# A conditioned transformer block on one core: earlier input, a new first tile, two banks and new orders at the end

## What is computed

```python
def _tc_rmsnorm(x, t, gw, gb, bw, bb):
    g = (t @ gw.T + gb)[:, None, :]
    b = (t @ bw.T + bb)[:, None, :]
    inv_rms = jax.lax.rsqrt(jnp.mean(x * x, axis=-1, keepdims=True) + EPS)
    return g * x * inv_rms + b

def _attention(x, Wq, Wk, Wv, Wo):      # 16 heads of 16
    ...
    p = softmax(q @ k.T / sqrt(dh))
    return (p @ v) @ Wo.T

def _swiglu(x, gate_w, hid_w, out_w):   # 1024 hidden channels
    return jax.nn.silu(x @ gate_w.T) * (x @ hid_w.T) @ out_w.T

x1 = x + _attention(_tc_rmsnorm(x, t, g1w, g1b, b1w, b1b), Wq, Wk, Wv, Wo)
out = x + x1 + _swiglu(_tc_rmsnorm(x1, t, g2w, g2b, b2w, b2b), gate_w, hid_w, out_w)
```

## Time and profile before

| | us |
|---|---|
| median of 3 runs | 942.82 (942.0 to 943.25) |
| the profiled execution | 944.17 |
| span of its instructions | 942.4 |
| TensorE (PE) busy in that span | 898.8, 95% |
| DVE, ACT, POOL busy | 629.0, 553.4, 493.3 |
| mean granted TensorE clock | 0.981 of full speed |

### The profile page before, as it was taken

One profiled execution on the slowest core, in us unless ns is written; L12 is line 12 of the kernel. 1 busy time (PEld: TensorE's weight loads), 2 busy tenths in 40 slices (PEclk: granted clock), 3 DMA queues, 4 the chain that ended last, 5 costly groups with the idle time before them and its releaser, 6 DMA issues.

```text
span 942.4 us, 22491 instructions
## 1 busy us (share of the span) xinstructions
PE 898.8 (95%) x8988; PEld 772.6 (82%) x8988; DVE 629.0 (67%) x1067; ACT 553.4 (59%) x1255; POOL 493.3 (52%) x409
## 2 busy tenths in 40 slices
PE   4668999999999999999999999999999999999998
PEld 3556888888888888888888888888888888888887
DVE  3537758586875848687585867758586775857642
ACT  4456657565665757566565756656565665655541
POOL 4554737365473736547373654727365472735433
PEclk9769999999999999999999999999999999999999
DMA  5300102020110201011020101102010110100000
GB/s 194 101 24 23 35 18 64 1 58 24 46 35 11 71 1 57 24 46 35 5 77 1 56 26 45 35 2 80 2 55 26 47 35 1 58 1 24 2 23 23
DMA packets 25672, 35.13 MB, mean 37 GB/s; under 512 B 3296, under 2 KB 20896, under 8 KB 25440
## 3 DMA queue, kind: packets, MB, share of 16 engines
q1 hardware_dynamic: 25344, 33.59, 11.8%
q10 hardware_dynamic: 224, 0.10, 0.0%
HBM read 25.27 MB, written 8.42 MB: 36 GB/s over the span
## 4 chain that ended last, share of the span: by engine, by line
PE 87%; DVE 5%; ACT 4%; issue 3%; DMA 1%; POOL 0%; SPq 0%; DVEq 0%; ACTq 0%; POOLq 0%
PE ps L1084 9%; PE ps L1086 9%; PE ps L1085 9%; PE ps L1220 7%; PE ps L1226 6%; PE ps L1221 6%; PE ps L1236 6%; PE ps L1239 5%; PE ps L1237 5%; PE ps L1192 5%; PE ps L1207 4%; PE ps L1112 4%; PE ps L1115 3%; PE ps L1113 3%; PE ps L1182 2%
## 5 line engine op out<-in xcount | busy, mean ns | idle before, releaser
L293 POOL TENSOR_TENSOR h_lo<-h,h_hi 128x512 fp32r<-128x512 f32 x128 | 164.2, 1291 | 179.3 <-ACT h_hi L522 179.3
L299 POOL TENSOR_TENSOR probs<-probs,recip 128x512 f32<-128x512 f32 x128 | 131.8, 1045 | 56.1 <-DVE recip L829 56.1
L840 DVE SCALAR_TENSOR_TENSOR shared<-shared,ps 128x512 f32<-128x512 f32 x128 | 85.5, 668 | 97.2 <-ACT shared L517 97.2
L1084 PE MATMUL ps<-out_w_hi,h_hi 128*128 128x256 f32 x512 | 144.8, 283 | 0.0
L1086 PE MATMUL ps<-out_w_hi,h_lo 128*128 128x256 f32 x512 | 144.7, 283 | 0.0
L1085 PE MATMUL ps<-out_w_lo,h_hi 128*128 128x256 f32 x512 | 144.2, 282 | 0.0
L847 DVE SCALAR_TENSOR_TENSOR h<-shared,ps 128x512 f32<-128x512 f32 x128 | 87.4, 683 | 32.4 <-issue 22.1
L1220 PE MATMUL ps<-xn_hi,gate_w_hi 128*128 128x512 f32 x256 | 106.3, 415 | 2.6 <-ACT xn_hi L488 2.0
L532 ACT COPY probsT<-ps 128x512 f32<-128x512 f32 x128 | 69.2, 590 | 65.5 <-PE ps L1192 65.5
L517 ACT ACTIVATE shared<-ps 128x512 f32<-128x512 f32 x128 | 76.2, 595 | 53.5 <-PE ps L1226 52.6
L1236 PE MATMUL ps<-xn_hi,hid_w_hi 128*128 128x512 f32 x256 | 106.2, 415 | 0.0
(11 more groups left out here) (92 smaller groups left out, 2016.2 us busy)
## 6 DMA issues: line engine op xcount, KB each, us to landing
x_in<-in_x SPq DMA_DIRECT2D x16, 512.0 KB, 3.8
xT_in<-in_xT SPq DMA_DIRECT2D x16, 512.0 KB, 3.4
out<-result SPq DMA_DIRECT2D x15, 512.0 KB, 3.7
inv_all<-inv_rows SPq DMA_DIRECT2D x15, 256.0 KB, 4.0
shared<-in_attT SPq DMA_DIRECT2D x1, 1024.0 KB, 8.4
shared<-in_gateT SPq DMA_DIRECT2D x1, 1024.0 KB, 10.3
shared<-in_hidT SPq DMA_DIRECT2D x1, 1024.0 KB, 4.9
shared<-in_outT SPq DMA_DIRECT2D x1, 1024.0 KB, 5.4
```

The source lines that it names most:

```text
L293: nc.gpsimd.tensor_tensor(h_lo[:, j % KEPT, :], h[:, j % 2, :], h_hi[:, j % KEPT, :].bitcast(F32), ALU.subtract).then_inc(h_lo_done, 1)
L299: nc.gpsimd.tensor_tensor(own, own, recip[:, p % TOGETHER, :].unsqueeze(2).to_broadcast([P, SEQS, L]), ALU.mult).then_inc(divided, 1)
L1084: nc.tensor.matmul(dst, a_hi, b_hi, start=first, stop=False, skip_group_check=skip)
```

## The change

- The input: `keep_input` goes; SP loads x a second time, straight into `x_res`, when `sum_of_inputs` of the tile before has read it. `x_in` and `xT_in` of the next tile are loaded as soon as their squares and scaling are done, the first ones before the hidden weights. SP's list per iteration has a new order.
- The start: TensorE spreads the factors before it makes gains and shifts; DVE scales the first tile into PSUM banks 6 and 7 and does gain and shift for both channel halves there (`whole_norm1`); ACT rounds the value and output attention weights after the first input.
- The first tile: gate, hidden and output weights are rounded and subtracted in halves, spread over new lists of steps on every engine. The first queries move from ACT to DVE, the second keys and second queries from DVE to ACT (`other_keys`, `other_queries`). `scores(t, 1)` now follows the two halves of `project_v`, and `project_q(t + 1, 0)` comes ahead of the last two transposes.
- Behind the last tile: gate and hid products alternate between two banks each (`gate_bank`, `hid_bank`), so that they wait for chunk j - 2; the result's first half is released after half of the last `down` (`first_down`).
- New orders in `last_tile` and `after_last` on all four engines.

The steady tiles' lists are the same on TensorE, DVE and POOL; ACT's lacks `keep_input`.

```diff
@@ sync @@
+            sp.wait_ge(ms1_done, 1)
+            sp.dma_start(x_in[:, :, :], x_t[1]).then_inc(x_loaded, 16)
+            sp.wait_ge(scaled1, 1)
+            sp.dma_start(xT_in[:, :, :], xT[1]).then_inc(xT_loaded, 16)
+            sp.dma_start(x_res[:, :, :], x_t[0]).then_inc(x_res_loaded, 16)
+
             sp.wait_ge(w_split, 2)
             sp.dma_start(raw[:, 0, :].rearrange("p (c n) -> p c n", c=CH),
                          hidT.rearrange("(c p) n -> p c n", p=P)).then_inc(hid_w_in, 16)
 
-            sp.wait_ge(w_split, 3)
-            sp.dma_start(raw[:, 1, :].rearrange("p (j n) -> p j n", j=CHUNKS),
-                         outT.rearrange("(j p) n -> p j n", p=P)).then_inc(out_w_in, 16)
+            def next_factors(t):
+
+                sp.wait_ge(inv1_done, t + 2)
+                sp.dma_start(inv1_rows, inv1[:, :]).then_inc(inv1_out, 16)
+                sp.wait_ge(inv1_out, 16 * t + 16)
+                sp.dma_start(inv1_all[:, :], inv1_rows.rearrange("p k -> (p k)").unsqueeze(0).to_broadcast([P, TOK])
+                             ).then_inc(inv1_in, 16)
 
             def iteration(t, attend, mlp, finish, ahead):
-                if ahead:
-
-                    sp.wait_ge(scaled1, t + 1)
-                    sp.dma_start(xT_in[:, :, :], xT[t + 1]).then_inc(xT_loaded, 16)
-                if finish and (attend or mlp):
-
+                if alone(t):
+                    next_factors(t)
+                    sp.wait_ge(w_split, 4)
+                    sp.dma_start(raw[:, 1, :].rearrange("p (j n) -> p j n", j=CHUNKS),
+                                 outT.rearrange("(j p) n -> p j n", p=P)).then_inc(out_w_in, 16)
+                elif attend:
+                    if ahead:
+                        sp.wait_ge(ms1_done, t + 1)
+                        sp.dma_start(x_in[:, :, :], x_t[t + 1]).then_inc(x_loaded, 16)
+                        sp.wait_ge(scaled1, t + 1)
+                        sp.dma_start(xT_in[:, :, :], xT[t + 1]).then_inc(xT_loaded, 16)
+                    sp.wait_ge(sum_done, t)
+                    sp.dma_start(x_res[:, :, :], x_t[t]).then_inc(x_res_loaded, 16)
+                    if finish:
+                        sp.wait_ge(result_done, 2 * (t - 1))
+                        sp.dma_start(out_t[t - 2], result[:, :, :]).then_inc(stored, 16)
+                    if ahead:
+                        next_factors(t)
+                elif mlp:
                     sp.wait_ge(result_done, 2 * (t - 1))
                     sp.dma_start(out_t[t - 2], result[:, :, :]).then_inc(stored, 16)
-                if finish and not (attend or mlp):
-
+                else:
                     for half in range(2):
                         blocks = slice(2 * half, 2 * half + 2)
                         sp.wait_ge(result_done, 2 * (t - 1) - 1 + half)
                         sp.dma_start(out_t[t - 2, :, blocks, :], result[:, blocks, :]).then_inc(stored, 16)
-                if ahead:
-
-                    sp.wait_ge(x_res_done, t + 1)
-                    sp.wait_ge(ms1_done, t + 1)
-                    sp.dma_start(x_in[:, :, :], x_t[t + 1]).then_inc(x_loaded, 16)
-
-
-                    sp.wait_ge(inv1_done, t + 2)
-                    sp.dma_start(inv1_rows, inv1[:, :]).then_inc(inv1_out, 16)
-                    sp.wait_ge(inv1_out, 16 * t + 16)
-                    sp.dma_start(inv1_all[:, :], inv1_rows.rearrange("p k -> (p k)").unsqueeze(0).to_broadcast([P, TOK])
-                                 ).then_inc(inv1_in, 16)
 
...
@@ vector: the first tile's normalisation @@
+            def whole_norm1():
+
+                for c in range(CH):
+                    scaled = ps[:, PAIR + 2 + c, :].rearrange("p (b q) -> p b q", q=L)
+                    last = nc.vector.tensor_tensor(scaled, scaled, of_sequences(0, c, 0), ALU.mult)
+                last.then_inc(gained1, 1)
+                dve.wait_ge(gained1, 1)
+                for c in range(CH):
+                    nc.vector.tensor_tensor(xn1[:, c, :].rearrange("p (b q) -> p b q", q=L),
+                                            ps[:, PAIR + 2 + c, :].rearrange("p (b q) -> p b q", q=L),
+                                            of_sequences(1, c, 0), ALU.add).then_inc((xn1_first, xn1_second)[c], 1)
+
...
@@ tensor: first tile @@
@@ -1290,21 +1360,21 @@
                 u = t - 1
                 project_k(0, 1)
                 scores(t, 0)
+                project_q(0, 1)
                 project_v(0, 1)
                 project_v(0, 0)
+                scores(t, 1)
                 transpose_probs(t, 0)
-                project_q(0, 1)
-                scores(t, 1)
                 transpose_probs(t, 1)
                 transpose_probs(t, 2)
                 transpose_probs(t, 3)
                 values_probs(t, 0)
                 transpose_probs(t, 4)
                 transpose_probs(t, 5)
+                project_q(t + 1, 0)
                 transpose_probs(t, 6)
                 transpose_probs(t, 7)
                 values_probs(t, 1)
-                project_q(t + 1, 0)
                 project_q(t + 1, 1)
                 project_k(t + 1, 0)
...
@@ scalar: first tile @@
             def first_tile(t, ahead):
                 u = t - 1
-                keep_input(t)
+                squares1(t + 1)
+                high_gate_weights(0)
+                first_keys(t)
+                other_keys(t)
+                high_gate_weights(1)
                 exp(t, 0)
-                high_hid_weights()
+                high_hid_weights(0)
                 exp(t, 1)
+                exp(t, 2)
+                other_queries(t)
+                high_hid_weights(1)
+                first_values(0)
                 keep_transposed(t, 0)
-                exp(t, 2)
                 exp(t, 3)
-                squares1(t + 1)
-                first_values(0)
+                second_norm1(t + 1)
+                keep_transposed(t, 1)
                 exp(t, 4)
-                exp(t, 5)
-                exp(t, 6)
-                keep_transposed(t, 1)
-                keep_transposed(t, 2)
-                high_out_weights()
-                keep_transposed(t, 3)
-                exp(t, 7)
-                keep_transposed(t, 4)
-                high_attention(t, 0)
-                keep_transposed(t, 5)
-                second_norm1(t + 1)
                 high_norm1(t + 1, 0)
                 high_norm1(t + 1, 1)
+                exp(t, 5)
+                keep_transposed(t, 2)
+                keep_transposed(t, 3)
+                high_attention(t, 0)
+                exp(t, 6)
+                keep_transposed(t, 4)
+                exp(t, 7)
+                keep_transposed(t, 5)
                 keep_transposed(t, 6)
                 keep_transposed(t, 7)
+                high_out_weights(0)
+                high_out_weights(1)
                 high_attention(t, 1)
                 first_keys(t + 1)
...
@@ tensor: two banks @@
@@ -1210,33 +1276,35 @@
                 last.then_inc(pv_mm, 1)
 
             def gate(u, j):
-                wait(pe, silu_done, CHUNKS * u + j)
+                wait(pe, silu_done, CHUNKS * u + (max(j - 1, 0) if ends(u) else j))
+                dst = ps[:, gate_bank(u, j), :]
                 if j == 0:
                     if alone(u):
-                        pe.wait_ge(w_split, 5)
...
@@ tensor: last tile @@
                 hid(u, 3)
                 transpose_probs(t, 2)
                 transpose_probs(t, 3)
+                gate(u, 4)
+                scores(t, 1)
                 down(u, 0)
-                scores(t, 1)
-                down(u, 1)
-                gate(u, 4)
                 hid(u, 4)
+                gate(u, 5)
                 values_probs(t, 0)
                 transpose_probs(t, 4)
-                gate(u, 5)
+                down(u, 1)
                 down(u, 2)
+                hid(u, 5)
                 transpose_probs(t, 5)
-                hid(u, 5)
-                gate(u, 6)
                 transpose_probs(t, 6)
                 transpose_probs(t, 7)
                 hid(u, 6)
                 values_probs(t, 1)
+                gate(u, 6)
+                project_out(t, ahead)
                 gate(u, 7)
-                project_out(t, ahead)
                 hid(u, 7)
                 down(u, 3)
                 down(u, 4)
...
@@ vector: result in halves @@
 
             def results(u):
                 if isinstance(u, int) and u < 0:
                     return
-                dve.wait_ge(down_mm, CHUNKS * (u + 1))
+                if ends(u):
+                    dve.wait_ge(first_down, 1)
+                else:
+                    dve.wait_ge(down_mm, CHUNKS * (u + 1))
                 dve.wait_ge(sum_done, u + 1)
                 wait(dve, stored, 16 * u)
                 for half in range(2):
+                    if ends(u) and half:
+                        dve.wait_ge(down_mm, CHUNKS * (u + 1))
```

(80 more changed lines are left out.)

200 lines of the change are left out of this document (102 added, 98 removed).

## The result

| | before | after |
|---|---|---|
| median, us | 942.65 (942.0 to 943.25) | 931.33 (931.1 to 933.37) |
| ratio | 1 | 0.9885 [0.9868, 0.9902] |
| span of the profiled execution | 942.4 | 929.3 |
| mean granted clock in it | 0.981 | 0.989 |

The change saves 11.3 us (1.15%); I had forecast 19.5 and the range ended at 930.5, so the prediction was wrong: the time lies 0.8 us beyond the range and 8.0 above the forecast of 923.3. In every run here the device time is the span plus 1.8 us, so spans can be compared directly.

The account below looks back on a forecast made before the run. TensorE was taken as the bound, busy 54.77 of 55 us in a steady tile, with 32.9 us idle in the first 82. Terms -16.0 - 2.1 - 0.8 - 0.6 = -19.5 off 942.8 gave 923.3 us, range 919.5 to 930.5.

Parts of the forecast that it names:

- the steady tiles at nothing: Steady tiles: dropped copies, x_res by DMA and earlier loads cost 0 us, as TensorE covers them; bounds 0 to -3.
- rival 5: Second tile: the gains of the start are lost to waits there, no change in time; chance 0.02.
- rival 4: Steady tiles: x_res arrives after project_out and holds first_residual, 15 tiles 1.5 us late, 945 us; chance 0.02.
- The base: Whole kernel: gains summed on a span of 942.4 us, then taken off the median of 942.8.
- rival 1: Start stalls anew: half speed until project_out, or POOL or hidden weights late; 926 to 930 us; chance 0.23.
- Start: First tile up to the first gate product: 16.0 us gained, bounds 11 to 17.5.
- the tie with project_out's first half: First tile: POOL's low output weights let first_residual go at 54.3 us, just as project_out's first half ends.
- Last tile and behind it: Last tile 46.9 us against 49.0, gain 2.1; feed-forward behind it gains 0.8, the split result 0.6.
- the three terms: End of the kernel: last tile 2.1 us, feed-forward behind it 0.8, result released in halves 0.6.
- Rival 2: The end gives nothing, waits only move elsewhere; the start alone gives 926.8 us; chance 0.10.
- Rival 3: First tile: the walk is too careful, the second scores start warm; 919 to 921 us; chance 0.08.

Follow-up runs that it names:

- before_input: The kernel before with only the input part (x_res by DMA, SyncE's new load order, no `keep_input`), old start and end: 946.49 us, ratio 1.005.
- x_after_xT: The changed kernel with the next tile's two loads swapped, xT_in first and then x_in: 925.64 us, ratio 0.9818.
- norm_sbuf: The changed kernel with the first tile's scaled input in SBUF (`xn1`) instead of PSUM: 931.61 us, ratio 0.9874.
- old_end: The changed kernel with the old orders in `last_tile` and `after_last`, one bank for each kind, result in one piece: 933.75 us, ratio 0.9914.
- pool_hid_later: The changed kernel with GpSimd's first low half of the hidden weights behind division 3 instead of ahead of it: 929.03 us, ratio 0.9854.

## Why the prediction was wrong, point by point

**The step that failed: the steady tiles at nothing**, with bounds of 0 to -3. I asked of every moved transfer whether its reader would be late, and none was. What I left out is what the transfer displaces: SyncE's order in each iteration puts the load of x_in directly behind the broadcast, 3.5 us ahead of a burst of 256 TensorE instructions that are themselves fetched by DMA. Measured: 1.6 + 2.2 us of standing and 1.9 us around them, most of it half speed behind the second, 5.7 us over 55.1 a tile and 5.5 over before; `before_input` loses by it on its own, `x_after_xT` wins it back. That "TensorE covers it, with 0.2 us idle per tile" was the wrong reading: a full engine has no slack to cover with, anything that touches it adds to the time. The earlier trace rows gave the DMA share as a mean over a tile (0.12); the share in the microseconds of the burst was the one to ask for. The text did name "a steady tile has got longer" as what would prove it wrong, but no rival had a mechanism or a chance for it: rival 5 put lost gains into the second tile alone, and rival 4 feared the load of x_res, which never was late.

**The base.** The sum was made against the profiled execution (942.4 + 1.8 = 944.2), and I took it off the median, 942.8. That is 1.4 us of the miss. Of the eighteen runs of before beside the experiments, the three with a mean clock of 0.981 have spans of 941.8, 941.9 and 942.3, the fifteen with 0.985 to 0.987 lie at 939.5 to 941.7. The profiled execution had 0.981: it is one of the long kind, and the sum's gain over it was in part one that the median had already. Where in the kernel it lies is not shown; the start, where half speed comes and goes, is my guess. By spans the change brought 13.1, by medians 11.3.

Of the 8.0 us between 923.3 and 931.33, 5.5 are the steady tiles, 1.4 the base, 0.8 the start, 0.1 the end, and 0.2 the median of after over its profiled execution. The steady tiles alone would have left the time at 928.8, inside a range drawn that wide for rival 1; a hit by it would have been luck.

**Start: right in mechanism, 15.2 for 16.0.** project_k at 16.90 (forecast 16.95) with pitches of 0.42 to 0.56 us at first, not yet 0.23; the two gains took 1.30 and the two shifts 1.29 (I had put 0.62 each with one wait); second scores 30.86 (forecast 30.2). Then the mis-sized term: division 3 was to end at 37.8 and ended at 40.9. Division 2 was already late (35.7 for 34.4); the other 2 us are DVE's shift, which took 2.72 us, not 0.7, beside POOL's `low_hid_weights(0)`. I had put half a weight ahead of division 3 on POOL and counted its own time there, but nothing for DVE beside it, though the same pair stood in the earlier trace rows at 2.74. That rule of the Trainium skill ("SBUF — State Buffer", "Who interferes with whom"), which I used for the first normalisation only, held at both places: 2.72 against 0.69 when the pair was parted, and 2.35 against 1.30 for the gains of `norm_sbuf`. After that values_probs(0) at 42.78 (41.1) and (1) at 50.70 (48.7), project_out at 54.64 (52.7, or 54.5 with the hand-overs, which was right), first gate product 66.45 (65.5). POOL's low output weights ended at 56.4, as the tie with project_out's first half had it.

**Last tile and behind it: right.** The wait before `values_probs` is 0.4 us, the 0.6 before the transposes is gone, the tile takes 47.1 us to the first gate product behind it (46.9 forecast, 49.0 before); from there the last product ends after 34.15 us, at 926.0 (33.9 forecast, 34.9 before). DVE's additions and the stores after it:

```profile
925.32 1.41 DVE L911 TENSOR_TENSOR result<-ps,x_plus_x 128x512 f32<-128x512 f32 x2 [4.43 <-PE ps L1152]
...
926.04 1.09 SPq L271 DMA_DIRECT2D out<-result  x2
```

The first addition starts 0.7 us ahead of the last product's end (925.72 + 0.29), so only one stands behind it, against both in the earlier trace rows: from the last product to the end 3.3 us, where before took 4.1. By the two profiles the three terms are then 1.9, 0.75 and 0.7 us, for 2.1, 0.8 and 0.6. `old_end` tests the three together only.

**Rivals.** Rival 1 (the start stalls anew, 926 to 930) has a number near the result and the wrong place: half speed did come back in the start, `values_probs(0)` took 1.93 us against 1.10 of the second, but the sum had most of that. Its argument that half speed holds for the whole of the middle of before was a wrong reading: the granted clock there is 0.50 from 37 to 57 us and again from 61 to 67, but 1.00 between. Rival 2 (the end gives nothing) is refuted by `old_end`. Rival 3 (second scores warm) came in part: they took 1.54 us, not 2.0, but began no earlier, and the transposes behind them ran slow again (1.97). For rivals 4 and 5: no engine waited for x_res, and the second tile lost 1.9 us by the stall, not by waits on other engines.

## What to carry to other kernels

- When a load is moved, list what else uses the DMA engines in the microseconds after its new issue; TensorE's own instructions are among them. A burst of small matmuls uses a 16 KB packet of them in 2 to 3 us, and a bulk load issued just ahead of it can stop the engine that has no slack.
- In an unbroken steady state, "hidden" has to be argued by the wait that the cover leaves, not by the engine's share: the same transfer cost 5 us when issued 3.5 us ahead of the burst and nothing when issued 1 us behind it.
- Take the sum and the base from the same execution, and compare its granted clock with that of the other runs first.

## What the runs showed of the hardware that I had not expected

TensorE can stand for 1.3 to 2.2 us with no semaphore that the profile shows to wait for, and the profile calls this "issue". A packet of its instructions, which in before began to move within 0.4 us of the scores, began 1.7 to 2.6 us after them beside a load that in after held the DMA share at 0.7 to 1.0. It hit the same two tiles of fourteen in all six profiled executions (five kernels) with that order of loads, those in which in before the packet ended only 1.5 and 1.6 us ahead of its use. The Trainium skill ("Runtime: NRT & Kernel Launch", "Instruction fetch mechanics") says that an engine fetches its instructions in blocks of 256 (16 KiB) over a DMA queue of its own, and that crossing from one to the next is mostly hidden. The size agrees with the 71 packets here (18205 records, 256 each). That the crossing is hidden holds in before for all tiles, but with this order of loads for twelve of the fourteen only, and the measurement decides.

A standstill of 2.2 us was followed by about 3 us at a granted clock of 0.50 in after, and so were the four of 1.96 to 2.20 us at this place in other kernels; one of 1.4 us in `pool_hid_later`, at the same place, was followed by none, nor were the six of 1.3 to 1.8 us in the second tile. Length alone does not decide: the wait of 2.05 us before the first gate product was followed by half speed in `x_after_xT` (at 68 to 70 us) and not in after.
